# Fewer, larger transfers of gather index lists in the attention pass of a graph network

## The chip, the core and the metric

The kernel runs on one core of one Trainium2 chip. The metric is the device time of one execution in microseconds (us). The engines go by short names: PE (TensorE, matmuls), DVE (VectorE), ACT (ScalarE), POOL (GpSimd, which issues the gathers here) and SP (SyncE, which issues other transfers). Each engine works through its own list of instructions in order, and the lists are tied together by semaphores: a wait holds back everything that stands behind it in the same list.

## The reference

Four graph layers are applied one after the other to 12500 nodes of 64 features, over 200000 edges sorted by destination node; each is added to its input and normalised. Only the first, graph attention, is touched. Cut to what matters:

```python
h = (x @ W).reshape(N, H, D)                       # N=12500, H=4, D=64
src, dst = edges plus one self loop for each node
alpha = leaky_relu(a_src[src] + a_dst[dst], 0.2)   # one score per edge and head
alpha = softmax of alpha over the edges of each dst
msg = h[src] * alpha[:, :, None]
out = segment_sum(msg, dst, num_segments=N).reshape(N, H * D) + bias
x = layernorm(x + out @ Wl + bl)
```

## The kernel before

The four layers are run as seven passes over the edges; pass 0, "gat", is the attention layer. The edges are cut into 392 **groups** of 512 (GE, four columns of 128), and pass 0 treats them in 49 **rounds** of eight groups, one for each of the eight **slots** of the gather buffer. The group 8i+s stands in slot s of round i. As the edges are sorted by destination, a group touches one tile of 128 nodes or a few (lo to hi in the code). When the last group of a block of seven tiles is summed, DVE, PE and ACT turn to the nodes of that block (the DVE lines 1165 and 1304 to 1312, among others) before they take the next group.

For one group g the engines do this:

- **SP** (`feed`, called as `feed(0)`) issues two small transfers. `load_idx` (L520 to L522) brings the group's source numbers, 128 partitions by four int32, into its slot of `idx`; it waits until DVE has given the slot free (`slots_free`, so until group g-8 is summed). `load_dst` (L515 to L517) brings the group's row of 512 destination numbers, the same row to all 128 partitions, into one of two places of `dstb`; it waits for `dstb_free`, which DVE raises at L1563 once the earlier row in that place is used up. In SP's list the two alternate: the list of group g+5 (AHEAD = 5, L53), then the row of group g+1.
- **POOL** (`gather_all`, L660 to L669) waits for the slot to be free and for the group's list (`idx_loaded[s]`), and then issues four indirect transfers (L655 to L657), one for each of the four columns of 128 edges. Each fetches 128 rows of the table `table_gat`, picked by `idx`, into the slot. Each adds 16 to `gathered[s]` when it has landed.
- **DVE** (`one_round` in `pass_vector`, L1553 on) waits for `expand_open` (L1562), raises `dstb_free` (L1563), waits for its slot's gathers (L1564), adds the gathered scores to the destination's (L1565), applies the leaky maximum (L1568) and the shift (L1570). Then `spread_dst(s + 1)` (L1541 to L1548) waits for the dst row **of the next group** and compares it with the node numbers (L1547, one instruction per tile of nodes): these are the one-hot matrices from which PE spreads node values to the next group's edges. Then follow the weights (L1575), the messages (L1576, L1582), and `sum_last` (L1514), which adds the sums of the group before to the accumulator and raises `slots_free` (L1538). So the slot of group g is given free in the step of group g+1.
- **PE** spreads node values to edges with `expand` (L846 to L857), fills pauses with matmuls on zeros (L791), and sums messages by destination in `aggregate` (L807 to L818).
- **ACT** loads the edge features of the group (L1069) and computes the exponentials and the other one-hot matrices (L1074, L1077).

Eight slots let POOL run up to seven groups ahead of DVE. The dst rows have two places, so SP can hold one row ahead. The other six passes build their index lists on DVE and gather in another function; they use none of the lines named here.

Of the kernel before, what the change touches and what calls it, by code (L numbers as in the profile page):

```python
# [25 lines left out]
C = 4  # L26
GE = P * C
SLOTS = 8
ROUNDS = -(-N_EDGES // (GE * SLOTS))
# [20 lines left out]
COLS = GROUPS * C  # L50
ROUND_COLS = SLOTS * C
TURN_SHARE = (1 << 16) // TB + 1
AHEAD = 5  # L53
PIECES = [14, 14, 14, 7] * 2
PIECE_AT = [sum(PIECES[:j]) for j in range(len(PIECES))]
SRC_HALF = TILES // 2
# [31 lines left out]
def build(nc, x, edge_attr, src_r, dst_r, dst_b, src_c, dst_c, w, out):  # L88
    ctx = ExitStack()
    with ctx:  # L90
        def sb(name, shape, dt=F32):
            return ctx.enter_context(nc.sbuf_tensor(name, shape, dt))

        def sem(name):
            return ctx.enter_context(nc.semaphore(name))
# [12 lines left out]
        slots_free = {parts: sem(f"slots_free_{parts}") for parts in (1, 3)}  # L108
        gathered = {parts: [sem(f"gathered_{parts}_{s}") for s in range(SLOTS)] for parts in (1, 3)}
# [40 lines left out]
        more_ready, more_free = sem("more_ready"), sem("more_free")  # L150
        counts_stored, stage_free, most_in, most_red = sem("counts_stored"), sem("stage_free"), sem("most_in"), sem("most_red")
        info_ready, build_over = sem("info_ready"), sem("build_over")
        idx_loaded = [sem(f"idx_loaded_{s}") for s in range(SLOTS)]
        rows_free, rows_cut, messages_ready = sem("rows_free"), sem("rows_cut"), sem("messages_ready")
        hot_in, hot_distance = sem("hot_in"), sem("hot_distance")
        score_sum, score_leaky, weight_rest = sem("score_sum"), sem("score_leaky"), sem("weight_rest")
# [61 lines left out]
        idx = sb("idx", [P, SLOTS, C], I32)  # L218
# [187 lines left out]
        def settle(eng):  # L406

            eng.sem_inc(waits_passed, 1)
# [97 lines left out]
        def _(sp):  # L506
# [3 lines left out]
            def feed(k):  # L510

                ps = passes[k]

                def load_dst(s, g):

                    sp.wait_ge(dstb_free, g + 1)
                    sp.dma_start(dstb[:, s % 2, :], dst_b[bass.ds(g, 1), :].rearrange("a e -> (a e)").partition_broadcast(P)).then_inc(dstb_loaded[s % 2], 16)  # L517

                def load_idx(s, g):

                    sp.wait_ge(ps["slots_free"], g + 1)
                    sp.dma_start(idx[:, s % SLOTS, :], src_r[:, bass.ds(g * C, C)]).then_inc(idx_loaded[s % SLOTS], 16)  # L522

                load_dst(0, 0)
                for s in range(AHEAD):
                    load_idx(s, s)
                with sp.Fori(0, ROUNDS - 1) as i:
                    for s in range(SLOTS):
                        load_idx(s + AHEAD, i * SLOTS + (s + AHEAD))
                        load_dst(s + 1, i * SLOTS + (s + 1))  # L530
                for s in range(SLOTS):
                    if s + AHEAD < SLOTS:
                        load_idx(s + AHEAD, (ROUNDS - 1) * SLOTS + s + AHEAD)
                    load_dst(s + 1, (ROUNDS - 1) * SLOTS + s + 1)

            def build_sync(sp):
# [78 lines left out]
            with sp.If(wide(sp) > 0):  # L615
                with sp.Fori(0, GROUPS) as g:
                    sp.wait_ge(max_free, g + 1)
                    sp.dma_start(idx[:, 0, :], src_r[:, bass.ds(g * C, C)]).then_inc(max_loaded, 16)
                    sp.dma_start(max_dstb, dst_b[bass.ds(g, 1), :].rearrange("a e -> (a e)").partition_broadcast(P)).then_inc(max_loaded, 16)
            feed(0)  # L620
            build_sync(sp)
            for k in range(1, len(passes)):
                if passes[k]["parts"] == 1:
                    feed(k)
                else:
                    feed_dense(k)
# [3 lines left out]
        def _(pool):  # L630
# [23 lines left out]
            def gather(ps, s):  # L654

                for c in range(C):
                    pool.indirect_dma_start(ps["buf"][:, s, c, 0:ps["row"]], None, ps["table"][:, :],  # L657
                                            bass.IndirectOffsetOnAxis(idx[:, s, c:c + 1], 0)).then_inc(ps["gathered"][s], 16)

            def gather_all(k):  # L660

                ps, order = passes[k], full_order[k]
                pool.wait_ge(table_done, 16 * tables_before[k])
                with pool.Fori(0, ROUNDS) as i:
                    for s in range(SLOTS):
                        pool.wait_ge(ps["slots_free"], i * SLOTS + (order * GROUPS + s + 1))
                        pool.wait_ge(idx_loaded[s], i * 16 + (order * ROUNDS * 16 + 16))
                        settle(pool)
                        gather(ps, s)  # L669

# [25 lines left out]
            taken_slots = pool.alloc_register("pool_taken")  # L696
            pool.reg_mov(taken_slots, 0)
            gather_all(0)
            build_pool()
            pool.wait_ge(info_ready, 1)  # L700
            for k in range(1, len(passes)):
                if passes[k]["parts"] == 1:
                    gather_all(k)
                else:
                    gather_cold(k)
# [1209 lines left out]
```

## Time and profile before

| | |
|---|---|
| median of 3 runs | 10603.79 us (10591.12 to 10607.39) |
| the profiled execution | 10593.45 us |
| its span in the trace | 10591.6 us |
| PE, DVE, POOL, ACT busy | 68%, 47%, 43%, 17% of the span |
| mean granted clock of PE | 0.804 of full speed |

The span goes from the first to the last recorded instruction of the one execution that the hardware profiler took; the execution's own time is a little longer. The names of the trace are the kernel's: `ARENA` is one large buffer in which the gather slots, the messages, `dstb` and others lie, `table_gat` the table that is gathered from, `idx<-src_r` the transfer of an index list, `ARENA<-dst_b` that of a dst row. A queue such as SPq or DVEq stands for an engine's issuing of transfers or semaphore steps. In a timeline, a row ends with the engine's idle time before the instruction and what ended it.

### The profile page before, as it was taken

Reading aid. Unit: us, or ns where it says so; the run is one execution under the profiler, and the core shown is the slowest. Engines: PE = TensorE matmul, PEld = TensorE weight load, DVE = VectorE, ACT = ScalarE, POOL = GpSimd, SP = SyncE. Lnnn points to the kernel's source line nnn. Section 1 sums busy time; section 2 is a strip of 40 time slices with the busy share of each in tenths; the row PEclk is TensorE's granted clock in tenths of the full one; section 3 lists DMA queues with packets and bytes.
Section 4 is the critical chain, followed back from the end, with each engine's and each line's share of the span. In section 5 each row is a group of like instructions: output and inputs, shape, how many; then the busy total and the mean of one; then the engine's idle time right before and its main releaser. Section 6 shows DMA issues by size and latency. Waiting matters only on the chain.

```text
span 10591.6 us, 264936 instructions
## 1 busy us (share of the span) xinstructions
PE 7210.5 (68%) x70314; PEld 5219.5 (49%) x70315; DVE 4954.3 (47%) x13673; ACT 1823.6 (17%) x3608; POOL 4603.7 (43%) x4467
## 2 busy tenths in 40 slices
PE   5888788777736666667778766666776555555676
PEld 4666566555512221114445455555665444444666
DVE  4555555444478777774443333333233332322433
ACT  2333333333202335540000000000000000000000
POOL 3777666554400000007540064436444664543754
PEclk7899888888868889997889877776777776667777
DMA  3444333333301122335555655555556666556666
GB/s 67 97 95 89 89 85 83 82 80 74 69 29 49 73 97 121 133 158 157 164 166 178 205 192 180 187 203 172 200 199 217 222 237 220 176 200 223 202 227 219
DMA packets 973363, 1566.12 MB, mean 148 GB/s; under 512 B 499841, under 2 KB 621441, under 8 KB 966402
## 3 DMA queue, kind: packets, MB, share of 16 engines
q1 hardware_dynamic: 485762, 1244.14, 33.2%
q0 software_dynamic: 150016, 196.43, 9.1%
q10 hardware_dynamic: 337280, 122.87, 4.5%
q14 instruction: 283, 2.32, 0.1%
q8 instruction: 22, 0.36, 0.0%
HBM read 1337.91 MB, written 225.00 MB: 148 GB/s over the span
## 4 chain that ended last, share of the span: by engine, by line
PE 41%; issue 18%; DVE 17%; DVEq 13%; DMA 6%; POOL 3%; ACT 2%; SPq 0%; ACTq 0%; POOLq 0%
PE ps_turn L970 19%; PE ps_out L818 6%; PE ps_turn L926 4%; DMA ARENA<-counts 4%; POOL ARENA L657 3%; DVE onehots L1780 3%; DVEq L1794 2%; PE ps_pair L818 2%; PE ps_turn L791 2%; DVE ARENA L1698 2%; DVE ARENA L1700 2%; DMA ARENA<-edge_attr 2%; PE ps_pair L998 1%; PE ps_turn L729 1%; PE ps_out L733 1%
## 5 line engine op out<-in xcount | busy, mean ns | idle before, releaser
L970 PE MATMUL ps_turn<-ARENA 128*128 128x192 bf16 (+2 forms) x28812 | 2708.3, 260 | 550.6 <-issue 200.3
L970 PEld LDWEIGHTS ps_turn<-ARENA 128*128 128x128 bf16 x28812 | 2266.9, 104 | 986.7 <-issue 675.6
L657 POOL DMA_INDIRECT ARENA<-table_sage,idx x1920 | 1901.2, 990 | 1615.6 <-DVE idx L1775 1076.7
L657 POOL DMA_INDIRECT ARENA<-table_gat,idx x1568 | 1732.0, 1105 | 1048.3 <-DMA idx<-src_r 559.8
L998 PE MATMUL ps_pair<-ARENA,onehots 128*128 128x64 bf16 (+2 forms) x12168 | 820.7, 225 | 1097.3 <-DVE ARENA L1787 962.1
L926 PE MATMUL ps_turn<-ARENA 128*128 128x392 bf16 (+1 forms) x4204 | 1064.5, 360 | 677.3 <-DVE ARENA L1700 353.4
L998 PEld LDWEIGHTS ps_pair<-ARENA,onehots 128*128 x12168 | 671.1, 116 | 1253.3 <-issue 1250.5
L657 POOL DMA_INDIRECT ARENA<-table_dev,idx x480 | 475.0, 990 | 1757.6 <-DVE idx L1775 1620.7
L1698 DVE TENSOR_SCALAR ARENA<-ARENA 128x784 bf16<-128x784 f16 (+1 forms) x2102 | 1007.3, 479 | 362.4 <-issue 233.0
L1826 DVE TENSOR_REDUCE DSUM<-ps_turn 128x64 f32<-128x192 f32 (+2 forms) x686 | 264.7, 386 | 1947.8 <-PE ps_turn L970 1838.7
L1780 DVE SCALAR_TENSOR_TENSOR onehots<-DST,TBASE,COL 128x512 f32 x1014 | 763.5, 753 | 652.7 <-issue 651.3
L926 PEld LDWEIGHTS ps_turn<-ARENA 128*128 128x128 bf16 (+1 forms) x4204 | 338.4, 101 | 1403.2 <-issue 1358.2
L657 POOL DMA_INDIRECT ARENA<-table_gine,idx x480 | 476.7, 993 | 1011.2 <-DVE idx L1775 876.5
L1132 ACT ACTIVATE ARENA<-ps_turn 128x784 f32 x784 | 645.2, 823 | 1085.3 <-PE ps_turn L926 1084.9
L791 PE MATMUL ps_turn<-ZEROS 128*128 128x128 bf16 x6762 | 572.1, 226 | 239.1 <-issue 185.4
L791 PEld LDWEIGHTS ps_turn<-ZEROS 128*128 128x128 bf16 x6762 | 438.8, 101 | 376.5 <-issue 340.5
L818 PE MATMUL ps_out<-ARENA,onehots 128*128 128x320 f32 x1568 | 569.7, 515 | 0.0
L1074 ACT ACTIVATE tmp<-COL,dst_in 128x128 bf16<-128x128 f32 x1568 | 501.1, 390 | 257.2 <-issue 257.2
L1700 DVE TENSOR_SCALAR ARENA<-ARENA 128x128 bf16<-128x128 f16 (+1 forms) x2102 | 519.6, 247 | 0.0
L818 PE MATMUL ps_pair<-ARENA,onehots 128*128 128x320 f32 x1568 | 515.7, 476 | 0.0
L1576 DVE TENSOR_TENSOR ARENA<-ARENA 128x1024 f32<-128x1024 f32 x392 | 477.0, 1217 | 0.0
L1547 DVE TENSOR_SCALAR ARENA<-ARENA,NODE 128x512 bf16<-128x512 int32 x489 | 252.8, 517 | 472.1 <-PE ps_pair L853 258.4
(296 smaller groups left out, 5865.9 us busy)
## 6 DMA issues: line engine op xcount, KB each, us to landing
ARENA<-counts SPq DMA_DIRECT2D x1764, 448.0 KB
counts<-ARENA SPq DMA_DIRECT2D x49, 3136.0 KB, 9.0
ARENA<-counts SPq DMA_DIRECT2D x588, 224.0 KB
ARENA<-dst_b SPq DMA_DIRECT2D x393, 256.0 KB
ARENA<-edge_attr ACTq DMA_DIRECT2D x392, 128.0 KB
ARENA<-table_sage,idx POOLq DMA_INDIRECT x1920
ARENA<-table_gat,idx POOLq DMA_INDIRECT x1568
nodes_dev<-table_rows ACTq DMA_DIRECT2D x14, 672.0 KB
```

The lines of the kernel that those rows point to most:

```text
L657: pool.indirect_dma_start(ps["buf"][:, s, c, 0:ps["row"]], None, ps["table"][:, :], bass.IndirectOffsetOnAxis(idx[:, s, c:c + 1], 0)).then ...
L791: pe.matmul(ps_fill, ZERO[:, :], ZERO[:, :], start=True, stop=True)
L818: last = pe.matmul(sums[:, 0:MSGW if gat else n], lhs, rhs, start=(c == 0 and q == 0), stop=(c == C - 1 and q == parts - 1))
L926: last = pe.matmul(ps_turn[:, at:at + WIDE_ROW // 2], marks[:, 0:P], marks[:, P + q * (WIDE_ROW // 2):P + (q + 1) * (WIDE_ROW // 2)], star ...
L970: last = pe.matmul(ps_dense[half][:, 0:n], RING[:, b, :], XP[:, b, :], start=(b == PIECE_AT[pieces[0]]), stop=(j == pieces[-1] and b == PI ...
L998: last = pe.matmul(sums, hot[:, c * P:(c + 1) * P], buf[:, s, c, q * n:(q + 1) * n], start=(c == 0 and q == 0), stop=(c == C - 1 and q == 2))
L1074: act.activation(distance[:, c * P:(c + 1) * P], COL[:, :], ACT.Abs, scale=-1.0, bias=dst_in[:, s % 2, c:c + 1]).then_inc(hot_distance, 1)
L1132: act.activation(to[:, :, c * CHUNK:(c + 1) * CHUNK].rearrange("p (q b) v -> p q b v", q=2), sums.rearrange("p q (b v) -> p q b v", v=CHUN ...
L1576: ve.tensor_tensor(msg[:, s % 2, :, 0:H * D].rearrange("p c (h d) -> p c h d", h=H), buf[:, s, :, 0:D].unsqueeze(2).broadcast_to([P, C, H, ...
L1698: ve.tensor_scalar(marks[:, P:P + WIDE_ROW], IOTA16, BASES[:, bass.ds(q, 1)], KEY_pad[:, bass.ds(j, 1)], ALU.add, ALU.is_equal).then_inc(r ...
L1700: ve.tensor_scalar(marks[:, 0:P], COL16, AKEY_pad[:, bass.ds(j, 1)], None, ALU.is_equal).then_inc(ready, 1)
L1780: return ve.scalar_tensor_tensor(ring, DST[:, bass.ds(cols, C)].unsqueeze(2).broadcast_to([P, C, P]), TBASE[:, bass.ds(t, 1)], COL[:, :].u ...
```

## The change

SP brings index lists four groups at a time: one transfer for slots 0 to 3, one for slots 4 to 7 of a round, 98 in all in place of 392. There are two semaphores `idx_loaded`, one for each half. Before SP refills a half for round i+1 it waits until the gathers of all four groups of round i that read that half have landed (`gathered`, in place of the wait for `slots_free`). The first half is refilled ahead of the dst row of group 8i+1, the second ahead of that of group 8i+4; the dst rows themselves keep their order and their waits. Before the loop, SP waits once for `slots_free` and brings both halves of round 0. POOL waits for a list only at slots 0 and 4.

```diff
--- before.py
+++ after.py
@@ -50,7 +50,6 @@
 COLS = GROUPS * C
 ROUND_COLS = SLOTS * C
 TURN_SHARE = (1 << 16) // TB + 1
-AHEAD = 5
 PIECES = [14, 14, 14, 7] * 2
 PIECE_AT = [sum(PIECES[:j]) for j in range(len(PIECES))]
 SRC_HALF = TILES // 2
@@ -150,7 +149,7 @@
         more_ready, more_free = sem("more_ready"), sem("more_free")
         counts_stored, stage_free, most_in, most_red = sem("counts_stored"), sem("stage_free"), sem("most_in"), sem("most_red")
         info_ready, build_over = sem("info_ready"), sem("build_over")
-        idx_loaded = [sem(f"idx_loaded_{s}") for s in range(SLOTS)]
+        idx_loaded = [sem(f"idx_loaded_{h}") for h in range(2)]
         rows_free, rows_cut, messages_ready = sem("rows_free"), sem("rows_cut"), sem("messages_ready")
         hot_in, hot_distance = sem("hot_in"), sem("hot_distance")
         score_sum, score_leaky, weight_rest = sem("score_sum"), sem("score_leaky"), sem("weight_rest")
@@ -516,21 +515,28 @@
                     sp.wait_ge(dstb_free, g + 1)
                     sp.dma_start(dstb[:, s % 2, :], dst_b[bass.ds(g, 1), :].rearrange("a e -> (a e)").partition_broadcast(P)).then_inc(dstb_loaded[s % 2], 16)
 
-                def load_idx(s, g):
-
-                    sp.wait_ge(ps["slots_free"], g + 1)
-                    sp.dma_start(idx[:, s % SLOTS, :], src_r[:, bass.ds(g * C, C)]).then_inc(idx_loaded[s % SLOTS], 16)
+                def load_idx(h, i):
+
+                    sp.dma_start(idx[:, 4 * h:4 * h + 4, :].rearrange("p s c -> p (s c)"),
+                                 src_r[:, bass.ds(i * ROUND_COLS + 4 * C * h, 4 * C)]).then_inc(idx_loaded[h], 16)
+
+                def reload_idx(h, i):
+
+                    for q in range(4):
+                        sp.wait_ge(ps["gathered"][4 * h + q], i * (16 * C) + 16 * C)
+                        settle(sp)
+                    load_idx(h, i + 1)
 
                 load_dst(0, 0)
-                for s in range(AHEAD):
-                    load_idx(s, s)
+                sp.wait_ge(ps["slots_free"], 1)
+                for h in range(2):
+                    load_idx(h, 0)
                 with sp.Fori(0, ROUNDS - 1) as i:
                     for s in range(SLOTS):
-                        load_idx(s + AHEAD, i * SLOTS + (s + AHEAD))
+                        if s in (0, 3):
+                            reload_idx(s // 3, i)
                         load_dst(s + 1, i * SLOTS + (s + 1))
                 for s in range(SLOTS):
-                    if s + AHEAD < SLOTS:
-                        load_idx(s + AHEAD, (ROUNDS - 1) * SLOTS + s + AHEAD)
                     load_dst(s + 1, (ROUNDS - 1) * SLOTS + s + 1)
 
             def build_sync(sp):
@@ -664,7 +670,8 @@
                 with pool.Fori(0, ROUNDS) as i:
                     for s in range(SLOTS):
                         pool.wait_ge(ps["slots_free"], i * SLOTS + (order * GROUPS + s + 1))
-                        pool.wait_ge(idx_loaded[s], i * 16 + (order * ROUNDS * 16 + 16))
+                        if s % 4 == 0:
+                            pool.wait_ge(idx_loaded[s // 4], i * 16 + 16)
                         settle(pool)
                         gather(ps, s)
 
```

## Rows read from the trace of the kernel before

**Rows 1.** The profile page, its first line.
```profile
span 10591.6 us, 264936 instructions
```

**Rows 2.** Windows, POOL at L657: stretch, us, POOL busy (x), PEclk, DMA share, GB/s.
```profile
174.00:800.00 626.00, 489.74 (x448) 0.90 0.44 96
...
975.00:2950.00 1975.00, 1078.16 (x993) 0.86 0.36 80
```

**Rows 3.** Waits of POOL, 175 to 970 us: us, times, mean us.
```profile
POOL ARENA L657 <- DMA idx<-src_r: 2.4, 8, 0.3
```

**Rows 4.** Waits of POOL, 970 to 2950 us.
```profile
POOL ARENA L657 <- DMA idx<-src_r: 557.3, 116, 31.3
```

**Rows 5.** What line 1565 waits for, whole span: us, times.
```profile
  DMA ARENA<-table_gat,idx: 44.9, 27
```

**Rows 6.** Waits of all engines, 175 to 800 us.
```profile
DVE ARENA L1565 <- DMA ARENA<-table_gat,idx: 44.9, 27, 3.4
```

**Rows 7.** Timeline of SP's queue: start us, us, issue.
```profile
1185.68 0.33 SPq L522 DMA_DIRECT2D idx<-src_r  x1
...
1262.47 0.33 SPq L522 DMA_DIRECT2D idx<-src_r  x1
1262.99 0.64 SPq L517 DMA_DIRECT2D ARENA<-dst_b  x1
```

**Rows 8.** Timeline of POOL, four gathers; in brackets idle us before, and its releaser.
```profile
794.57 0.95 POOL L657 DMA_INDIRECT ARENA<-table_gat,idx  x1 [0.30 <-issue]
...
1188.12 1.61 POOL L657 DMA_INDIRECT ARENA<-table_gat,idx  x1 [5.30 <-DMA idx<-src_r]
...
1193.56 0.94 POOL L657 DMA_INDIRECT ARENA<-table_gat,idx  x1 [0.30 <-DVEq L1538]
...
1358.77 0.94 POOL L657 DMA_INDIRECT ARENA<-table_gat,idx  x1 [0.31 <-issue]
```

**Rows 9.** The chain of waits in order of time: start us, us, link.
```profile
209.99 5.42 DMA ARENA<-table_gat,idx
...
381.59 3.18 DMA ARENA<-table_gat,idx
...
827.08 3.24 DMA ARENA<-edge_attr
```

**Rows 10.** Timeline of DVE, lines 1547, 1565 and 1514.
```profile
371.01 0.49 DVE L1547 TENSOR_SCALAR ARENA<-ARENA,NODE 128x512 bf16<-128x512 int32 x1 [0.65 <-issue]
...
407.58 0.17 DVE L1565 TENSOR_TENSOR ARENA<-ps_pair,ARENA 128x16 f32<-128x16 f32 x1 [0.93 <-PE ps_pair L857]
...
734.54 0.60 DVE L1547 TENSOR_SCALAR ARENA<-ARENA,NODE 128x512 bf16<-128x512 int32 x1 [0.67 <-issue]
...
767.84 0.17 DVE L1565 TENSOR_TENSOR ARENA<-ps_pair,ARENA 128x16 f32<-128x16 f32 x1
...
782.84 0.52 DVE L1547 TENSOR_SCALAR ARENA<-ARENA,NODE 128x512 bf16<-128x512 int32 x1 [0.67 <-issue]
...
803.87 0.48 DVE L1514 TENSOR_TENSOR ARENA<-ARENA,ps_out 128x325 f32 x1
...
1195.56 0.48 DVE L1547 TENSOR_SCALAR ARENA<-ARENA,NODE 128x512 bf16<-128x512 int32 x1 [0.65 <-issue]
...
1267.47 0.62 DVE L1547 TENSOR_SCALAR ARENA<-ARENA,NODE 128x512 bf16<-128x512 int32 x1 [0.66 <-DMA ARENA<-dst_b]
...
1368.14 0.48 DVE L1547 TENSOR_SCALAR ARENA<-ARENA,NODE 128x512 bf16<-128x512 int32 x1 [0.67 <-issue]
```

**Rows 11.** Timeline of PE, two aggregations at line 818, eight matmuls each.
```profile
401.97 4.02 PE L818 MATMUL ps_out<-ARENA,tmp 128*128 128x320 f32 x8
...
407.64 2.40 PE L818 MATMUL ps_out<-ARENA,onehots 128*128 128x320 f32 x8
```

**Rows 12.** Windows of PE, columns as in rows 2 with PE busy.
```profile
402.60:406.00 3.40, 3.40 (x9) 0.50 0.24 44
406.00:412.00 6.00, 5.39 (x84) 1.00 0.40 90
```

## The prediction

> **What bounds the kernel now.** A change of 0.2%, some 21 us, is about what a measurement of this kernel can tell from none. The change lies in the attention pass alone, from 145 to 2950 us of a span of 10591.6 us [rows 1], so I read that stretch and asked of each queue who waits for it.
>
> First, POOL's gathers by stretch. From 174 to 800 us it issues 448 of them, 112 groups, in 626 us: one per 1.40 us, 5.59 us a group; from 975 us on it issues 993 in 1975 us and is busy for 55% of that [rows 2]. Second, POOL's waits: up to 970 us it waits 2.4 us in all for index lists, afterwards 557.3 us in 116 waits [rows 3, 4]. So in the first stretch POOL never runs dry and the lists lie there long before it comes to them; later it comes early and stands waiting for them. Third, does anyone wait for the gathers? DVE does at L1565: 44.9 us in 27 waits over the pass, and the same 44.9 us in the same 27 waits between 175 and 800 us [rows 5, 6]. After 800 us nobody waits for a gather. The pass thus has two halves: the first block of nodes, groups 0 to 111, paced by POOL's issue rate, with DVE close behind; and the rest, paced by PE and DVE, with gathers ready in advance.
>
> **What it removes.** 294 of SP's 392 index issues, 0.33 us each [rows 7]: SP otherwise waits, so nothing. Six of eight semaphore waits a round on POOL: its gap before a gather is 0.30 us inside a group too [rows 8], so nothing. The wait for a list: a gather could start up to 2.44 us earlier where POOL is idle (index issue 1185.68, gather 1188.12 [rows 7, 8]); nobody waits for those gathers, so nothing directly, and in the first block the lists are not late. I take 1.7 of the 2.44 us as what such a gather gains (below 0, above 2.44).
>
> A rule weighed here: the Trainium skill, "DMA: Bandwidth & Descriptors", section "Rules for kernel authors", says to coalesce small transfers, since under 64 KB one pays mostly overhead; its fixed cost of about 2 us, an estimate by that page, would make 294 transfers worth 588 us if they stood on the path. Rows 3 to 6 say that they do not; by the rows the sum takes nothing for them.
>
> **What it adds.** SP runs its list in order. Before load_dst(8i+4) it must now see the gathers of groups 8i+4 to 8i+7 landed, and before load_dst(8i+1) those of 8i to 8i+3. Queued behind the wait are exactly these dst rows, which DVE needs at L1547 while it is at group 8i+3 and 8i. DVE may no longer follow close behind POOL: at 8i+3 it has to wait until POOL has finished four groups more. (This cannot lock up: gather 8i+7 needs only the slot that DVE frees at 8i.)
>
> The path from POOL's last issue of group 8i+7 to DVE's L1547 has three pieces. Issue to landing of a gather: 3.18 to 5.42 us [rows 9]; I take 3.3, because the longer ones are the late ones that got onto the chain. SP, the list and then the dst row: 0.52 us between the two issues [rows 7], with the wake-up 0.7. The dst row's landing: its nearest lower row is the edge load, of half its bytes, 3.24 us [rows 9]; above, the one dst row that DVE ever waited for was issued at 1262.99 and used at 1267.47, 4.48 us [rows 7, 10]. I take 3.6, nearer to the lower, since the upper is the one late case of the pass. Sum: 7.6 us, bounds 7.0 and 10.6.
>
> **Term 1, the end of the first block.** Group 111's last gather is issued at 794.57 [rows 8]; so the dst row of 108 is there at 802.2 at the earliest. DVE wanted it at 782.84 [rows 10]: 19.3 us late. What follows to the end of group 111, last add 803.87 [rows 10], runs at DVE's and PE's own pace, and after 800 us there is no wait for gathers in which the lag could be won back. Less 1.5 us for short waits for PE that shrink behind a pause: 18 us (bounds 15 and 22). That every earlier round has such a pause costs nothing by itself, POOL being the pace there.
>
> **Term 2, POOL running dry.** It costs something if POOL finds no free slot. From its last issue for 8i+7 it has seven groups, 39.1 us, and that gather's own 1.25 us before it wants the slot of 8i+15, which DVE frees at 8i+8. DVE starts 7.6 us late and POOL restarts some 0.9 us after the release (an estimate, 2.6 less 1.7): that leaves DVE 31.9 us from L1547 of 8i+3 to the end of 8i+8. The rows give 36.6 us (371.01 to 407.58) and 33.3 us (734.54 to 767.84) [rows 10]; less the 3.3 us of gather waits that a round holds on average (44.9 us over 13.5 rounds), 33.3 and 30.0. So POOL falls dry by 1.4 us in rounds like the first and keeps 1.9 us in rounds like the second. I take 1 us a round over 13 rounds: 13 us (bounds 0 and 30).
>
> **Term 3, the rounds after.** Just behind the first block, DVE is 18 us late but POOL only some 9 (it has 9 us of queued groups to work off before it starves); at group 115 the dst row comes about 3 us late once more. From group 152 on, 29 rounds reload the second half. The distance from POOL's last issue of 8i+7 to DVE's L1547 of 8i+3 is 9.4 us in a round like that of 195 (1358.77 to 1368.14) and 2.0 us in that of 171 (1193.56 to 1195.56) [rows 8, 10]. 20 rounds have 7.5 us or more, eight 4.5 to 6.9. With the gather starting 1.7 us earlier 5.9 us are needed: 3.9 us are missing once and about 1.2 us five times, 10 us in all, of which PE's queued work hides a part. With the 3 us: 9 us (bounds 0 and 25, the latter at 10.6 us of path).
>
> **Term 4, the clock.** After the pause at a round's start TensorE's granted clock was 0.50, the 1.2 GHz level, and eight matmuls took 4.02 us; at 1.00, 2.4 GHz, the next eight took 2.40 [rows 11, 12]. New pauses bring more of that: hidden under POOL in the first block, 1.6 us at a few later ones, 3 us (0 and 10). The Trainium skill's "TensorE: Matmul & The Clock Gate", section "Why this matters for your kernels", warns of PE pauses between bursts of matmuls; the rows agree in kind, and by the rule taken for all 14 first-block pauses too, unhidden, the sum would be 22 us more.
>
> **Sum**: 18 + 13 + 9 + 3 = 43 us, all against. The profiled execution took 10593.45 us, so 10636 on that scale; it lies 10.3 us under the median of the runs shown, 10603.79, and against that median I say 10647 us.
>
> **Rivals.**
> *Faster: the list was the gathers' brake.* POOL's 557.3 us of waiting speak for it. If each of the 116 waits passed its 1.7 us on, that is 197 us, 10407. It decides only where DVE waits for gathers while POOL waits for lists, and the rows show no such moment [rows 4 to 6]. 6%. The coalescing rule of the Trainium skill points this way too.
> *No change that can be told.* The dst rows land at the lower bound, POOL never falls dry, PE's queue hides the later stalls: 15 us, 10619. For it: terms 2 and 3 are sums of 1 us margins. 14%.
> *Much slower.* The path is 10.6 us and POOL falls dry each round, 22 + 30 + 25 + 10 = 87 us, or beyond it, every later pause costs its half clock: 10691 and up. 4%.
> *The forecast*, dst rows behind the gathers: 76%.
>
> **How the numbers follow.** Slower by over 0.2%: forecast and much slower, 0.80; within 0.2%: 0.14; faster: 0.06. The range goes from 10612, below the no-change case, to 10691, where all upper bounds meet; it leaves out the faster case and the tail above.
>
> **What would show it.** Right: SP waits at the new lines for gathers, several hundred us; DVE waits at L1547 for ARENA<-dst_b in nearly every round before 820 us, where it now has none; its waits for gathers at L1565 go to almost none; group 112 begins 20 to 40 us later and the pass ends 35 to 55 us later; POOL's waits for idx are gone and replaced by waits for DVE. Wrong: dst_b ending no wait at L1547, or the first block ending at the same time, would fell terms 1 and 2; a pass that ends earlier, the whole reading.

## The result, and the profile after

The changed kernel is slower, by a little under half to two thirds of what was forecast.

| | median | before beside it | ratio, 95% interval |
|---|---|---|---|
| first measurement | 10620.16 us (10606.00 to 10647.42, 16 runs) | 10598.89 us (16 runs) | 1.0021 (1.0014 to 1.0029) |
| second measurement | 10622.96 us (10609.02 to 10641.15, 12 runs) | 10595.17 us (29 runs) | 1.0027 (1.0019 to 1.0036) |

As medians that is 21 and 28 us more; 43 us had been forecast. The profiled execution of the changed kernel took 10633.94 us, 14 us above its median, while that of the kernel before lay under its own. So the two profiles, read side by side, show more than the runs, 40.5 us; that this lies near the 43 forecast says nothing for the forecast. The profiles are good for the places of the loss, the timed runs for its size.

First SP's waits from 145 to 3000 us after the change (us in total, times, the longest). Line 516 is the dst row's issue, line 407 the helper behind the new waits for gathers.

```profile
SPq L516 <- DVEq L1570: 1912.3, 305, 34.4
SPq L407 <- DMA ARENA<-table_gat,idx: 544.8, 120, 31.3
```

SP now stands 544.8 us behind gathers, and each of these waits has a dst row behind it. DVE's waits from 145 to 830 us, the first block, have the answer to [rows 5, 6]:

```profile
DVE ARENA L1572 <- issue: 94.6, 35, 6.3
DVE ARENA L1554 <- DMA ARENA<-dst_b: 69.9, 14, 11.7
```

The waits for gathers (44.9 us in 27) are gone from the list, and 69.9 us in 14 waits for the dst row stand in their place, at the comparison that was L1547 and is L1554 now. (The other line, idle time that no event in the profile ends, is hardly changed: 100.2 us in 29 before.) POOL's waits from 170 to 830 us:

```profile
POOL ARENA L663 <- issue: 143.0, 419, 15.6
POOL ARENA L663 <- DVEq L1545: 29.7, 38, 5.5
```

No wait for a list is left, but POOL, which set the pace and had next to no wait of its own, now waits up to 5.5 us for a slot that DVE has not given free. It issues fewer gathers in the stretch of [rows 2], 438 against 448 in the same 626 us:

```profile
174.00:800.00 626.00, 480.36 (x438) 0.89 0.40 92
```

One pause in full, in round 12, from the timelines of POOL, SP and DVE (start, duration, instruction):

```profile
766.52 0.95 POOL L663 DMA_INDIRECT ARENA<-table_gat,idx  x1 [0.30 <-issue]
...
769.27 0.34 SPq L520 DMA_DIRECT2D idx<-src_r  x1
769.85 0.94 SPq L516 DMA_DIRECT2D ARENA<-dst_b  x2
...
774.28 0.49 DVE L1554 TENSOR_SCALAR ARENA<-ARENA,NODE 128x512 bf16<-128x512 int32 x1 [4.09 <-DMA ARENA<-dst_b]
```

POOL issues the last gather of group 103 at 766.52. SP sees it landed, sends the lists at 769.27 and at 769.85 the dst row of group 100 (x2: the row shows the issue of the next dst row with it). DVE, at group 99, has waited 4.09 us for it and goes on at 774.28. From gather to DVE that is 7.8 us; the forecast had put the path at 7.6. Read in the same way, all 42 pauses of the two profiles of the changed kernel have 6.6 to 8.7 us, with a median of 7.4: 2.8 from the gather's issue to SP's list, 0.6 to the dst row's issue, 3.8 from there to DVE (medians).

For the size of each stretch I take three starts of each profile: POOL's first gather of pass 0, DVE's scores of group 112 (the first of the next block of nodes) and of group 391 (the last). Of the kernel before:

```profile
145.92 23.27 POOL L657 DMA_INDIRECT ARENA<-table_gat,idx  x1 [15.58 <-issue]
...
817.56 0.17 DVE L1565 TENSOR_TENSOR ARENA<-ps_pair,ARENA 128x16 f32<-128x16 f32 x1 [8.02 <-issue]
...
2943.43 0.17 DVE L1565 TENSOR_TENSOR ARENA<-ps_pair,ARENA 128x16 f32<-128x16 f32 x1 [0.91 <-PE ps_pair L857]
```

and after the change, with the last gather and the last sum of group 111 between them:

```profile
149.33 23.24 POOL L663 DMA_INDIRECT ARENA<-table_gat,idx  x1 [15.61 <-issue]
...
810.46 0.94 POOL L663 DMA_INDIRECT ARENA<-table_gat,idx  x1 [0.30 <-issue]
...
843.08 0.49 DVE L1521 TENSOR_TENSOR ARENA<-ARENA,ps_out 128x325 f32 x1 [1.23 <-PE ps_out L825]
...
856.59 0.17 DVE L1572 TENSOR_TENSOR ARENA<-ps_pair,ARENA 128x16 f32<-128x16 f32 x1 [7.91 <-issue]
...
2984.96 0.17 DVE L1572 TENSOR_TENSOR ARENA<-ps_pair,ARENA 128x16 f32<-128x16 f32 x1 [0.91 <-PE ps_pair L864]
```

The first block, from gather to group 112, grew from 671.6 to 707.3 us; groups 112 to 391 took 2125.9 and now 2128.4. At the end of the block POOL's last gather is 12.5 us later than before (15.9, less the 3.4 by which the pass itself began later), and DVE's last sum comes 32.6 us behind that gather, where it came 9.3 us behind [rows 8, 10]: 23.3 us more of lag.

The same three starts in all profiles of this study; the last column is the timed ratio to the kernel before, with its 95% interval:

| kernel | first block, us | groups 112 to 391, us | ratio |
|---|---|---|---|
| before | 671.6 | 2125.9 | 1 |
| before, second profile | 673.1 | 2121.2 | no ratio, one run |
| after | 707.3 | 2128.4 | 1.0021 (1.0014 to 1.0029) |
| after, second profile | 699.0 | 2124.4 | 1.0027 (1.0019 to 1.0036) |
| wait_only | 719.4 | 2133.6 | 1.0059 (1.0046 to 1.0072) |
| first14 | 702.5 | 2112.7 | 1.0023 (1.0014 to 1.0032) |
| from14 | 664.0 | 2127.2 | 1.0001 (0.9993 to 1.0010) |
| mid | 686.1 | 2115.4 | 1.0002 (0.9993 to 1.0012) |
| late | 670.9 | 2113.6 | 0.9994 (0.9985 to 1.0003) |
| dbl | 672.2 | 2119.4 | 0.9990 (0.9981 to 0.9999) |
| dbl, second profile | 671.4 | 2107.6 | 0.9988 (0.9979 to 0.9997) |
| late_392 | 669.0 | 2118.0 | 1.0004 (0.9995 to 1.0013) |
| late_784 | 674.8 | 2112.8 | 1.0012 (1.0003 to 1.0021) |
| four_lists | 672.4 | 2134.1 | 1.0042 (1.0029 to 1.0056) |

Outside pass 0, where no kernel of the table differs from another, the profiles scatter too: from group 391 to the end of the span they take from 7646.5 to 7666.7 us. The first block repeats to 1.5 us in the two profiles of the kernel before and to 8 us in those of the changed one; 'late' and from14, which have the same instructions in it, differ by 6.9 us.

### The profile page after: what moved, and what is told of

Read it like the earlier page. It is cut to its first block, busy times and chain, and to the rows that moved or that the text cites. A ratio compares the mean times of both kernels' runs of the same rounds, so it can differ in the third digit from the quotient of the medians.

```text
span 10632.1 us, 264354 instructions
## 1 busy us (share of the span) xinstructions
PE 7232.4 (68%) x70314; PEld 5236.8 (49%) x70315; DVE 4952.4 (47%) x13673; ACT 1824.5 (17%) x3608; POOL 4585.0 (43%) x4467
## 4 chain that ended last, share of the span: by engine, by line
PE 42%; issue 18%; DVE 17%; DVEq 13%; DMA 7%; ACT 2%; POOL 1%; SPq 0%; ACTq 0%; POOLq 0%
PE ps_turn L977 19%; PE ps_out L825 6%; PE ps_turn L933 4%; DMA ARENA<-counts 4%; DVE onehots L1787 3%; PE ps_pair L825 3%; DVEq L1801 2%; PE ps_turn L798 2%; DVE ARENA L1707 2%; DVE ARENA L1705 2%; DMA ARENA<-edge_attr 2%; PE ps_pair L1005 1%; PE ps_turn L736 1%; POOL ARENA L663 1%; PE ps_out L740 1%
## 5 line engine op out<-in xcount | busy, mean ns | idle before, releaser
L1554 DVE TENSOR_SCALAR ARENA<-ARENA,NODE 128x512 bf16<-128x512 int32 x489 | 252.4, 516 | 534.7 <-PE ps_pair L860 253.3
```

## The experiments

My theory was the prediction's: the loss comes of dst rows that stand behind SP's waits for gathers. Its rivals were that the larger, later list transfers cost something of themselves, and that the lists had been a brake on the gathers after all.

**The changed kernel once more** (after_again), nothing edited.

> The changed kernel once more, for a second profile of it. The first one has pass 0 38 us longer than in the profile of the kernel before (34.5 at the end of the first block, 22 of them DVE's lag behind POOL and 12.5 POOL's own delay), while the timed medians stand only 21 us apart. If all three terms belong to the kernel, this profile has the first block 32 to 37 us longer again and the time is 10635; if POOL's delay varies from run to run, the lag is again 20 to 24 us, the delay anything from 0 to 15, and the time near 10620.

The first block took 699.0 us, 27 more than the mean of the two profiles of the kernel before (672.4). POOL's last gather and DVE's last sum of group 111 stand here:

```profile
805.90 0.95 POOL L663 DMA_INDIRECT ARENA<-table_gat,idx  x1 [0.30 <-issue]
...
834.60 0.48 DVE L1521 TENSOR_TENSOR ARENA<-ARENA,ps_out 128x325 f32 x1
```

The sum comes 28.7 us behind the gather (32.6 in the first profile, 9.3 before), so 19.4 us more of lag, and the gather is 8.0 us later than in the profile before, counted from the pass's first. Both parts vary by some 4 us: 23.3 and 19.4 us of lag, 12.5 and 8.0 us of POOL's delay. DVE's waits up to 830 us:

```profile
DVE ARENA L1554 <- DMA ARENA<-dst_b: 67.4, 13, 11.8
```

**The waits without the merging** (wait_only).

```diff
                         load_idx(s + AHEAD, i * SLOTS + (s + AHEAD))
+                        if s in (0, 3):
+                            for q in range(4):
+                                sp.wait_ge(ps["gathered"][4 * (s // 3) + q], i * (16 * C) + 16 * C)
+                                settle(sp)
                         load_dst(s + 1, i * SLOTS + (s + 1))
```

> The kernel before with its 392 list transfers left as they are, and only the waits for the gathers added ahead of the dst rows of groups 8i+1 and 8i+4. Theory 'dst rows behind the gathers': the whole loss comes back without any merging, 1.0015 to 1.004 of the kernel before, DVE waits for dst_b as in the changed kernel (about 70 us in 14 waits up to 830 us). Rival 'the merged transfers themselves cost or POOL suffers from lists that come in fours': no loss, within 0.0007 of before.

All of the loss is there with 392 transfers, and more than twice of it: 1.0059, some 62 us, where at most 1.004 was expected. The waits alone make it, without any merging. Why more? POOL's waits from 170 to 830 us, and DVE's from 145 to 830 us:

```profile
POOL ARENA L661 <- DMA idx<-src_r: 27.0, 41, 4.1
POOL ARENA L661 <- DVEq L1542: 5.8, 19, 0.3
```
```profile
DVE ARENA L1551 <- DMA ARENA<-dst_b: 82.0, 15, 10.9
```

Here the lists stand behind the same waits, one group at a time, and POOL runs dry for lists, 27.0 us in 41 waits; its last gather of the block comes 25.1 us later than before, where the change had 12.5 and 8.0. That the change pays less because one transfer then brings four groups' lists at once is an inference from these waits, not tested by itself: merging seems to soften the harm of the wait that merging itself needs.

**The refills behind the rows that they held up** (late).

```diff
                     for s in range(SLOTS):
-                        if s in (0, 3):
-                            reload_idx(s // 3, i)
                         load_dst(s + 1, i * SLOTS + (s + 1))
+                        if s in (3, 7):
+                            reload_idx(s // 4, i)
```

> The changed kernel with both refills moved in SP's list: that of the first half behind the dst row of group 8i+4, that of the second behind the dst row of 8i+8, so that the gathers waited for belong to the group at which DVE is anyway. Merged transfers and waits stay. Theory 'dst rows behind the gathers': the loss goes, within 0.0007 of the kernel before, no DVE waits for dst_b of note; POOL gets its lists about a group later than the slot in later rounds, which the slack of 15 us and more covers. Rival 'merged transfers': the loss stays at 1.002 or grows, the lists being later still.

The loss is gone: 0.9994, first block 670.9 us, no wait for dst_b in the whole pass. DVE's waits up to 830 us have their old form [rows 6] again:

```profile
DVE ARENA L1572 <- DMA ARENA<-table_gat,idx: 48.1, 33, 3.6
```

After 970 us POOL waits for lists as it did before, 193.1 us where it was 557.3 [rows 4], and to as little effect:

```profile
POOL ARENA L663 <- DMA idx<-src_r: 193.1, 34, 13.1
```

**Two sets of list slots** (dbl, and once more as dbl_again). The lists of round i+1 go into the other set, whose gathers landed a round ago; what orders them is the dst rows' own waits.

```diff
-        idx = sb("idx", [P, SLOTS, C], I32)
+        idx = sb("idx", [P, 2 * SLOTS, C], I32)
...
-                with sp.Fori(0, ROUNDS - 1) as i:
-                    for s in range(SLOTS):
-                        if s in (0, 3):
-                            reload_idx(s // 3, i)
-                        load_dst(s + 1, i * SLOTS + (s + 1))
+                with sp.Fori(0, ROUNDS // 2) as j:
+                    for u in range(2):
+                        i = j * 2 + u
+                        for s in range(SLOTS):
+                            if s in (0, 3):
+                                load_idx(1 - u, s // 3, i + 1)
+                            load_dst(s + 1, i * SLOTS + (s + 1))
```

(POOL's loop takes the two sets in turn in the same way, with a semaphore for each half of each set.)

> The changed kernel with two sets of eight list slots, used in turn, so that a refill writes lists of which the gathers landed a round ago, and SP waits for no gather at all; 98 transfers as in the change. Theory 'dst rows behind the gathers': within 0.0007 of the kernel before. Rival 'the lists were the gathers' brake': with the lists always there first, pass 0 would get shorter by tens of us (0.997 or less). Rival 'merged transfers cost': 1.002.

> The kernel with two sets of list slots once more: is it really faster than the one before? If merging by itself gains a little, the rest of pass 0 is again 5 to 13 us shorter than the 2126 us of before and the ratio 0.9985 to 0.9995; if not, 2120 to 2130 and 1.000.

0.9990 and 0.9988: the loss is gone here too, and both intervals end below 1. So with no harm from the waits, 98 transfers are worth a little, about 11 us, which the forecast had put at nothing. That the lists had been a brake on the gathers (0.997 or less) is ruled out. This version has the lowest ratio of the study, though its intervals overlap that of 'late'. A smaller part of the 'brake' is not told apart by this run alone, as its lists also come earlier.

**The change in the first block alone** (first14), **and after it alone** (from14). Two loops over the rounds in place of one, one with the refills as the change has them, the other as 'late'; here that of first14:

```diff
-                with sp.Fori(0, ROUNDS - 1) as i:
+                with sp.Fori(0, 14) as i:
                     for s in range(SLOTS):
                         if s in (0, 3):
                             reload_idx(s // 3, i)
                         load_dst(s + 1, i * SLOTS + (s + 1))
+                with sp.Fori(14, ROUNDS - 1) as i:
+                    for s in range(SLOTS):
+                        load_dst(s + 1, i * SLOTS + (s + 1))
+                        if s in (3, 7):
+                            reload_idx(s // 4, i)
```

> Merged lists throughout; the refills stand where the change puts them in rounds 0 to 13 (the first block of nodes), and behind the dst rows of 8i+4 and 8i+8 (as in the run 'late') from round 14 on. Theory 'the loss is made in the first block': block 1 is 27 to 36 us longer than before, as in the two profiles of the changed kernel, and from group 112 on the pass runs as in 'late', 2114 to 2119 us against 2124 to 2128; timed 1.0015 to 1.003. If the later rounds carry the loss as well, clearly less, under 1.001.

> The other way round: refills as in 'late' in rounds 0 to 13, as in the change from round 14 on. Prediction's terms 3 and 4 by themselves: block 1 as before (670 to 672 us), the rest of the pass 9 to 12 us longer than in 'late' (2114) and its twin with two sets of list slots (2119), so 2123 to 2130; timed 1.000 to 1.001. If the rounds after the first block cost nothing: 2114 to 2119 and 0.9985 to 0.9995.

first14 has the whole loss of the change, 1.0023, with its first block at 702.5 us and no wait for dst_b behind it; from14 has none, 1.0001. DVE's waits for dst rows, of first14 up to 830 us:

```profile
DVE ARENA L1559 <- DMA ARENA<-dst_b: 73.4, 14, 11.7
```

and of from14 from 812 to 2990 us:

```profile
DVE ARENA L1559 <- DMA ARENA<-dst_b: 27.3, 10, 10.2
```

Of these 27.3 us, 17.5 are two pauses at the switch itself (groups 112 and 115), of which the change has little, as DVE comes to that point late already. From 'late' to from14 the ratio rises by 0.0007, 7 us, about as much as the intervals leave open. From 'late' to first14 it rises by 0.0029, 31 us: so much the first block costs, in the runs as in the profiles (702.5 less 670.9).

**DVE two groups behind in place of four** (mid).

```diff
-                        if s in (0, 3):
-                            reload_idx(s // 3, i)
+                        if s in (2, 5):
+                            reload_idx(s // 5, i)
```

> The changed kernel with the first refill ahead of the dst row of 8i+3 (in place of 8i+1) and the second ahead of that of 8i+6 (in place of 8i+4): DVE may then trail POOL by two groups, not four. By the prediction's working the lag at the end of block 1 falls by two groups of 5.6 us, from 22 to about 11 us, and POOL, with two groups more in hand, never runs dry: block 1 is 8 to 13 us longer than before, the time 1.000 to 1.0015. If the loss came of any wait of SP for gathers, wherever it stands, it stays at 27 to 36 us.

The first block took 686.1 us, 13.7 more than the mean of before, a little more than expected and less than half of the change's 30.7 (mean of two profiles). POOL's waits for slots from 170 to 830 us are down to the usual 0.3 us each, so the part that came of POOL running dry is gone, and the lag is left, with fewer pauses of DVE:

```profile
POOL ARENA L663 <- DVEq L1545: 3.0, 10, 0.3
```
```profile
DVE ARENA L1554 <- DMA ARENA<-dst_b: 47.1, 10, 10.7
```

In time, 1.0002, it cannot be told from the kernel before.

**The kernel before once more** (before_again), nothing edited.

> The kernel before once more, for a second profile: how far do two profiles of the same kernel differ in pass 0? If the 6 to 18 us by which the later groups run shorter in 'late', 'first14' and the two runs with two sets of slots belong to the merged lists, the stretch from group 112 to the last is again near 2126 us here; if they are chance, it can be 2108 to 2120 as well. Block 1 670 to 673 us.

2121.2 us for the later groups against 2125.9: the two profiles differ by 5 us. The five of the merged kernels whose refills hold up no later dst row, or hardly one (first14, mid, late, dbl twice), lie at 2107.6 to 2119.4, below both. (So do late_392 and late_784 below, with 392 and 784 transfers.)

**Is it the number of transfers?** (late_392 and late_784.) 'late' with each refill sent as four, then as eight transfers; here the first:

```diff
-                    sp.dma_start(idx[:, 4 * h:4 * h + 4, :].rearrange("p s c -> p (s c)"),
-                                 src_r[:, bass.ds(i * ROUND_COLS + 4 * C * h, 4 * C)]).then_inc(idx_loaded[h], 16)
+                    for q in range(4 * h, 4 * h + 4):
+                        sp.dma_start(idx[:, q, :], src_r[:, bass.ds(i * ROUND_COLS + C * q, C)]).then_inc(idx_loaded[h], 16)
...
-                            pool.wait_ge(idx_loaded[s // 4], i * 16 + 16)
+                            pool.wait_ge(idx_loaded[s // 4], i * 64 + 64)
```

> The kernel 'late' with each refill sent as four transfers of one group each, 392 in all as in the kernel before, at the same place behind the same waits. If the number of list transfers is what 'late' gains by, its rest of the pass goes back from 2114 to about 2126 us and the ratio to 1.000; if the gain comes of the place or is chance, 2108 to 2119 us and 0.9985 to 0.9995.

> The same with eight transfers of half a group, 784 in all: the suspected cost twice as large. If each list transfer costs the pass as much as the 294 removed ones seem to give (10 us by 294, 0.034 us each), the rest of the pass is 13 us longer than in 'late_392', about 2139 us, and the ratio 1.0012; if not, as 'late_392' and 'late'.

The two measurements part here. In time the row is in order, 0.9994, 1.0004, 1.0012 for 98, 392 and 784 transfers, with intervals that touch; in the profiles the later groups take 2113.6, 2118.0 and 2112.8 us, in no order. In late_784 part of the time is another thing: the burst of eight issues stands ahead of a dst row, and in the first block DVE waits for it. Its waits for dst rows over the pass:

```profile
DVE ARENA L1555 <- DMA ARENA<-dst_b: 11.6, 6, 3.3
```

**Four times the lists** (four_lists): the kernel before, with three more copies of each list and no wait for gathers, each group's lists behind the dst row of its step.

```diff
+        idx_copies = [sb(f"idx_copy_{k}", [P, SLOTS, C], I32) for k in range(3)]
...
-                    sp.dma_start(idx[:, s % SLOTS, :], src_r[:, bass.ds(g * C, C)]).then_inc(idx_loaded[s % SLOTS], 16)
+                    for to in (idx, *idx_copies):
+                        sp.dma_start(to[:, s % SLOTS, :], src_r[:, bass.ds(g * C, C)]).then_inc(idx_loaded[s % SLOTS], 16)
...
-                        load_idx(s + AHEAD, i * SLOTS + (s + AHEAD))
                         load_dst(s + 1, i * SLOTS + (s + 1))
+                        load_idx(s + AHEAD, i * SLOTS + (s + AHEAD))
...
-                        pool.wait_ge(idx_loaded[s], i * 16 + (order * ROUNDS * 16 + 16))
+                        pool.wait_ge(idx_loaded[s], i * 64 + 64)
```

> The kernel before with every list brought four times (three of them into places that nothing reads), 1568 transfers in place of 392, and each group's lists issued right behind the dst row of the same step and not ahead of it, so that no dst row waits for the added issues and no gather is waited for. If a list transfer costs the pass some 0.03 us (98, 392 and 784 of them stood at 0.9994, 1.0004 and 1.0012), 1176 more cost 30 to 40 us: 1.003 to 1.004, and most of it in pass 0. If the number of list transfers costs nothing, as the profiles of 'late_392' and 'late_784' have it after group 112 (2118 and 2113 us), 0.999 to 1.001.

1.0042, 44 us for 1176 more transfers: 0.037 us each (0.026 to 0.050 by the interval). By that, if the price is the same for each, the 294 that the change takes away are worth 11 us (8 to 15), which is what 'dbl' gains. The place of the lists behind the dst row and the three added buffers are changed here too, and no run has them by themselves; late_392, with 392 lists behind dst rows, stands at 1.0004. DVE never waits for a dst row in this run. What grew in its profile are PE's waits for the edge features, from 145 to 2950 us:

```profile
PE ps_out L809 <- DMA ARENA<-edge_attr: 52.6, 69, 1.5
PE ps_pair L809 <- DMA ARENA<-edge_attr: 22.8, 33, 1.3
```

The kernel before has, over the same stretch:

```profile
PE ps_out L807 <- DMA ARENA<-edge_attr: 38.3, 60, 1.3
PE ps_pair L807 <- DMA ARENA<-edge_attr: 18.3, 27, 1.3
```

18.8 us more of waiting for edges. The profiled execution was the shortest of the five runs (10607.39 us, median 10633.62), and its pass 0 only some 10 us longer, so it does not show where all of the 44 us go. Nor did these waits shrink with fewer lists: 62.8 us in 'late', 54.4 in 'dbl', 56.6 before. That more transfers go with more time is measured in the timed runs, from 98 to 1568 of them; the profiles do not show it, and by which path the smaller number gains is open.

## Why the forecast was right in kind and one and a half to two times too large

**What bounds, and what the change does.** Right. The pass behaves as two halves, and the loss lies in the first: first14 has all of it, from14 none that can be told.

**The path.** Right, 7.4 us in the median of the 42 pauses against 7.6, and close in its parts: from the gather's issue to the dst row's 3.4 us (2.8 and 0.6; 3.3 and 0.7 were put), and from there to DVE 3.8 us (3.6 were put, between 3.24 and 4.48). The pause shown above, with 4.4 us in the last part, is one of the longer ones there.

**Term 1**, 18 us forecast for DVE's lag at the end of the block: 23.3 and 19.4 us by the last sums of the two profiles. The size is near, but its working named the wrong place, so part of that is luck. In neither profile did DVE wait for the dst row of group 108, in the last round. It was that late already: the last pause of the block came at group 99 in both profiles (774.28 above), and what DVE lagged then it still lagged at the end of the block.

**Term 2**, 13 us for POOL running dry: 12.5 and 8.0 us. It did not come as 1 us in each round but in a few of them, up to 5.5 us at once, so the size came out and not the pattern. mid, with two groups more in hand, has none of it, as its working says.

**Terms 3 and 4**, 12 us: only partly seen. After 830 us the pauses stand where they were forecast, 115, 171 and five or six smaller ones:

```profile
DVE ARENA L1554 <- DMA ARENA<-dst_b: 10.7, 7, 2.9
```

But the later groups took only 2.9 us more than before (means of two profiles each, 2126.4 and 2123.5), and from14, the two terms by themselves, is 7 us above 'late' in time, of which a part may belong to its two pauses at the switch. Against the five merged kernels named above (mean 2113.7) the change stands 12.7 us higher, as forecast, and against the kernel before hardly at all.

**The step that failed** is the first of the sum: of 294 list issues "SP otherwise waits, so nothing". It costed the time that they took on SP, and not what the transfers may do beside the others once they are under way. By the timed runs they were worth 11 us (0.10 to 0.12% in 'dbl', 0.037 us each in four_lists; 'late' has 6 us, with an interval that reaches 1). If the change gains as much, the waits cost 21 plus 11 to 28 plus 11, so 32 to 39 us, against 43 in the sum; the transfers give back 11, against nothing. The two halves by themselves agree: first14 is 31 us and from14 7 us above 'late', 38 us together. The first of these is terms 1 and 2 as forecast (31); the second is terms 3 and 4, for which 12 had been put. So the rest of the miss, 4 to 11 us, may be their size, which the intervals and the scatter of single profiles leave open. Of the clock in the first block nothing is to be seen: the granted clock there is 0.89 in the window shown above and 0.90 in [rows 2].

The coalescing rule of the Trainium skill ("DMA: Bandwidth & Descriptors", section "Rules for kernel authors") was weighed at nothing by the same step. By sign the timed runs agree with the rule: 98, 392 and 784 transfers at the same place stand in order, though the intervals overlap. The Trainium skill's fixed cost of about 2 us, which the same page states for transfers that GpSimd issues (section "Anatomy of one DMA — SWDGE (gpsimd) path"), is no measure of that gain: off the path that sets the end, one of SP's list transfers cost 0.037 us here, an estimate from four_lists.

**Rivals.** 'The list was the gathers' brake' is out: with the lists always there first ('dbl') the gain is 11 us, not 197. 'No change that can be told' had part of the truth, not by the means it named. 'Much slower' is out for the change, but near to what wait_only became (62 us).

## What to carry to other kernels

Where an engine issues several streams of transfers, a wait that one stream needs delays all that stand behind it: ask of each new wait what is next in that queue, who reads it and how close that reader follows. Here the wait could be moved behind the urgent transfer at no cost ('late'), or a second set of buffers took it away ('dbl'), and then the merging's own small gain was kept. Of removed transfers, ask for what they do to the others under way as well as for the issuing engine's time, and settle gains of 0.1% by many timed runs, not by two profiles.

## What the runs showed of the hardware that was not expected

A small list transfer, on a path that does not set the end of the pass, still had a price in the timed runs, some 0.037 us by four_lists. The queues' packets from 975 to 2950 us (packets, MB, share of 16 engines), first of the kernel before, then of 'late', then of four_lists, show how little of it is bytes:

```profile
q1 hardware_dynamic: 72144, 66.86, 13.6%
```
```profile
q1 hardware_dynamic: 44943, 66.34, 11.9%
```
```profile
q1 hardware_dynamic: 179280, 68.43, 15.6%
```

With 0.8% fewer bytes in 'late' than before (two dst rows fewer are issued in the window), the queue has 38% fewer packets and 1.7 points less of the 16 engines' time, 27201 packets for 537 us of engine time (0.017 of 16 times 1975 us), some 20 ns a packet. In four_lists 107136 more packets took 2.0 points more, 6 ns each. But the second profile of the kernel before has fewer points for the same packets:

```profile
q1 hardware_dynamic: 72144, 66.86, 13.0%
```

Against it the two differences are 1.1 and 2.6 points, 13 and 8 ns: more packets go with more engine time, and no fixed price for one comes out.
